# Mixtures taken out of PSUM two banks at a time, from a ring of three pairs, with the last bias among the matmuls

## The reference

```
x = x + L0(x)     # conditional 1x1: agg_w = einsum('bk,koi->boi', att, weight); out = agg_w @ x + att @ bias_k
x = x + L1(x)     # grouped convolution, 4 groups, 9 taps, pad 4, plus c_weight @ cond and a bias
x = x + L2(x)     # conditional 1x1, as L0 with its own weights
x = x + L3(x)     # conditional 1x1, as L0 with its own weights
att = softmax(gelu(gelu(cond @ W0 + b0) @ W1 + b1) @ W2 + b2)   # 8 shares for each sample and layer
```

## Time and profile before

| what | value |
|---|---|
| median of 3 runs | 484.26 us (484.23 to 484.34) |
| the profiled execution's own time | 484.1 us |
| span of its profile | 482.3 us |
| TensorE busy (matmul) | 473.2 us, 98% of the span |
| TensorE weight loads | 446.3 us, 93% |
| VectorE busy | 320.2 us, 66% |
| ScalarE busy | 248.5 us, 52% |
| GpSimd busy | 151.2 us, 31% |
| mean granted TensorE clock | 0.997 of full speed |

### The profile page before, as it was taken

How to read it: one execution, slowest core, us unless ns; L and a number is a source line. 1 busy time by engine, 2 the same in 40 slices (tenths; PEclk the granted TensorE clock), 3 DMA queues, 4 the chain that set the end, 5 groups by cost and what they waited for, 6 DMA issues and landing times.

```text
span 482.3 us, 17714 instructions
## 1 busy us (share of the span) xinstructions
PE 473.2 (98%) x8003; PEld 446.3 (93%) x8003; DVE 320.2 (66%) x409; ACT 248.5 (52%) x414; POOL 151.2 (31%) x151
## 2 busy tenths in 40 slices
PE   8989999999999999999999999999999999999996
PEld 7978999999999999999999999999999999999995
DVE  3548687767676876767687776767777676777424
ACT  5654445466544545654455466444545654455544
POOL 2935072324133322414331331333223142420110
PEclk9999999999999999999999999999999999999998
DMA  8696977676546476664746666464667746452224
GB/s 277 207 334 184 302 232 226 209 221 208 186 120 215 156 217 219 207 216 112 211 149 217 209 214 216 129 206 140 215 203 220 220 149 208 131 187 77 90 88 175
DMA packets 39244, 92.86 MB, mean 193 GB/s; under 512 B 4601, under 2 KB 25473, under 8 KB 35201
## 3 DMA queue, kind: packets, MB, share of 16 engines
q1 hardware_dynamic: 39168, 91.73, 60.5%
HBM read 53.95 MB, written 37.77 MB: 190 GB/s over the span
## 4 chain that ended last, share of the span: by engine, by line
PE 97%; DMA 1%; issue 1%; DVE 0%; SPq 0%; DVEq 0%
PE cv_ps L508 59%; PE aux_ps L488 18%; PE aux_ps L537 15%; PE cv_ps L444 2%; PE cv_ps L431 1%; DMA consts_sb<-in_consts_dram 1%; PE cv_ps L537 1%; PE aux_ps L431 1%; PE aux_ps L466 0%; DVE y_all L847 0%; DVE m_all L797 0%; PE aux_ps L455 0%; PE aux_ps L400 0%; SPq L318 0%; SPq L319 0%
## 5 line engine op out<-in xcount | busy, mean ns | idle before, releaser
L508 PE MATMUL cv_ps<-x_hi,conv_lo 32*128 32x512 f32 x1536 | 284.7, 391 | 0.0
L508 PE MATMUL cv_ps<-x_hi,conv_hi 32*128 32x512 f32 x1536 | 284.2, 389 | 0.0
L508 PE MATMUL cv_ps<-x_lo,conv_hi 32*128 32x512 f32 x1536 | 284.2, 391 | 0.0
L508 PEld LDWEIGHTS cv_ps<-x_lo,conv_hi 32*128 32x128 f32 x1536 | 172.5, 184 | 4.7
L508 PEld LDWEIGHTS cv_ps<-x_hi,conv_hi 32*128 32x128 f32 x1536 | 171.5, 183 | 5.6
L508 PEld LDWEIGHTS cv_ps<-x_hi,conv_lo 32*128 32x128 f32 x1536 | 172.4, 183 | 4.5
L779 DVE SCALAR_TENSOR_TENSOR x_lo<-cv_ps,d_all,x_hi 128x512 fp32r<-128x512 f32 x128 | 87.2, 744 | 132.4 <-ACT x_hi L626 132.4
L636 ACT ACTIVATE y_all<-aux_ps,e_all 128x512 f32<-128x512 f32 x122 | 74.0, 689 | 134.1 <-PE aux_ps L537 134.1
L626 ACT ACTIVATE x_hi<-cv_ps,d_all 128x512 fp32r<-128x512 f32 x128 | 77.5, 688 | 67.9 <-PE cv_ps L508 67.9
L488 PE MATMUL aux_ps<-x_hi,a_hi 32*128 32x512 f32 x512 | 99.5, 391 | 2.3 <-issue 2.3
L488 PE MATMUL aux_ps<-x_hi,a_lo 32*128 32x512 f32 x512 | 99.1, 388 | 0.0
(11 more groups left out here) (104 smaller groups left out, 455.5 us busy)
## 6 DMA issues: line engine op xcount, KB each, us to landing
x_sb<-in_x_dram SPq DMA_DIRECT2D x31, 1024.0 KB, 6.5
out_dram<-y_all SPq DMA_DIRECT2D x60, 512.0 KB, 7.4
a_rep<-a_pairs SPq DMA_DIRECT2D x64, 128.0 KB, 7.3
m_rep<-m_pairs SPq DMA_DIRECT2D x64, 128.0 KB, 6.1
out_dram<-y_all SPq DMA_DIRECT2D x8, 256.0 KB, 2.6
a_pairs<-a_all SPq DMA_DIRECT2D x1, 1920.0 KB, 12.4
m_pairs<-m_all SPq DMA_DIRECT2D x1, 1792.0 KB, 12.2
m_all<-in_mix_dram SPq DMA_DIRECT2D x2, 512.0 KB, 5.5
```

The source lines that it names most:

```text
L508: mm = pe.matmul(cv_ps[:, g, :], w[rows(g), j, :], a[n % 2][rows(g), q, s:s + T], start=(i == 0), stop=(i == steps - 1))
```

## The change

- The mixtures are taken out in pairs: pair r holds the mixtures 2r and 2r+1, in two neighbouring banks, and one instruction of 128x1024 takes both out once both are made. There are 12 pairs; ScalarE takes r = 0, 2, 4, 6, 7, 8 and 10, VectorE takes r = 1, 3, 5, 9 and 11.
- The ring has three pairs of banks, so six banks in place of seven (`MIX_RING` = 6). Mixture t waits for the pair of mixture t - 6.
- `bias_e` becomes a generator that runs as a fifth member of the round after the first 12 steps: four empty steps, then one matmul in each step. The second stop of the mixtures goes.
- `bias_d` is issued before TensorE waits for the shares, in place of between the two products of `attention`.
- The load of the convolution's weights is issued after the first save of the layer-0 weights.
- On GpSimd, `split_a0(0)` comes before the split of the convolution's weights in place of behind it.

```diff
-BY_SCALAR = [t % 2 == 0 or t in (9, 21) for t in range(MIXES)]
+TWO = 2
+BY_SCALAR = [r % 2 == 0 or r == 7 for r in range(MIXES // TWO)]
+E_BEHIND = 4
...
-        mix_ps = [*prep_ps, aux_ps[:, 2, :], aux_ps[:, 3, :], aux_ps[:, 0, :]]
-        MIX_RING = len(mix_ps)
+        mix_ps = [cv_ps[:, 2:4, :], cv_ps[:, 0:2, :], aux_ps[:, 2:4, :]]
+        MIX_RING = TWO * len(mix_ps)
...
         def mix_taken(t):
-            return mix_out_a if BY_SCALAR[t] else mix_out_v, sum(by == BY_SCALAR[t] for by in BY_SCALAR[:t + 1])
+            r = t // TWO
+            return mix_out_a if BY_SCALAR[r] else mix_out_v, sum(by == BY_SCALAR[r] for by in BY_SCALAR[:r + 1])
...
             sp.dma_start(w3_sb, w3.rearrange("p (k m) -> p k m", k=K)).then_inc(e_loaded, DMA)
-            sp.dma_start(conv_f[:], conv).then_inc(conv_loaded, DMA)
...
-            sp.wait_ge(*mix_taken(NOG - 2))
+            sp.wait_ge(*mix_taken(NOG - 1 - TWO))
             sp.wait_ge(*mix_taken(NOG - 1))
             save(a0_all, a0_dram, 0, 1, a0_saved[0])
+            sp.dma_start(conv_f[:], conv).then_inc(conv_loaded, DMA)
...
                     if MIX_RING <= t:
                         pe.wait_ge(*mix_taken(t - MIX_RING))
-                    elif t == MIX_RING - 1:
-                        pe.wait_ge(spread_ready, NL)
...
-            def bias_e(options):
+            def bias_e():
+                for _ in range(E_BEHIND):
+                    yield
+                pe.wait_ge(e_loaded, DMA)
+                pe.wait_ge(c2_att_ready, 1)
+                for n in range(1, NL):
+                    pe.matmul(e_ps, bias_sb[:, n, :], att_t[:, n, :], start=(n == 1), stop=False)
+                    yield
+                for k in range(K):
+                    mm = pe.matmul(e_ps, w3_sb[:, k, :], c2_att[:, k, :], start=False, stop=(k == K - 1))
+                    if k == K - 1:
+                        mm.then_inc(e_made, 1)
+                    yield
...
             fill(8)
+            bias_d()
             attention()
...
             in_turn(mixing, 3 * G)
             biases()
-            in_turn(mixing, 2 * G)
-            bias_e(range(0, 4))
-            in_turn(mixing)
-            bias_e(range(4, K)).then_inc(e_made, 1)
+            in_turn([*mixing, bias_e()])
...
-            def mix_evacuate(t):
-                act.wait_ge(mix_made, t + 1)
-                nc.scalar.activation(mix_columns(t), mix_bank(t), ACT.Identity).then_inc(mix_out_a, 1)
+            def mix_evacuate(r):
+                act.wait_ge(mix_made, TWO * (r + 1))
+                nc.scalar.activation(mix_columns(r), mix_banks(r), ACT.Identity).then_inc(mix_out_a, 1)
...
+            split_a0(0)
             pool.wait_ge(pool_chain, PH)
             nc.gpsimd.tensor_copy(conv_hi[:], conv_f[:]).then_inc(conv_split, 1)
...
-            split_a0(0)
             split_a0(1)
...
-            def mix_evacuate(t):
-                dve.wait_ge(mix_made, t + 1)
-                nc.vector.tensor_copy(mix_columns(t), mix_bank(t)).then_inc(mix_out_v, 1)
+            def mix_evacuate(r):
+                dve.wait_ge(mix_made, TWO * (r + 1))
+                nc.vector.tensor_copy(mix_columns(r), mix_banks(r)).then_inc(mix_out_v, 1)
```

More of the change, by code:

```diff
@@ L236, in cond_resid_kernel, with mix_banks, mix_columns @@
         RING = len(prep_ps)
-        mix_ps = [*prep_ps, aux_ps[:, 2, :], aux_ps[:, 3, :], aux_ps[:, 0, :]]
-        MIX_RING = len(mix_ps)
[L242 to L247, removed]
+        mix_ps = [cv_ps[:, 2:4, :], cv_ps[:, 0:2, :], aux_ps[:, 2:4, :]]
+        MIX_RING = TWO * len(mix_ps)
+        def mix_banks(r):
+            return mix_ps[r % len(mix_ps)].rearrange("p u c -> p (u c)").rearrange("p (x b o) -> p b x o", x=TWO * G, b=B)
+        def mix_columns(r):
+            layer, u = TWO * r // NOG, TWO * r % NOG
             to = a0_all if layer == 0 else a23_all[layer - 1]
-            return to[:, :, OG * u:OG * (u + 1)].rearrange("p b (j o) -> p b j o", j=G)
+            return to[:, :, OG * u:OG * (u + TWO)].rearrange("p b (x o) -> p b x o", x=TWO * G)
         def mix_taken(t):
-            return mix_out_a if BY_SCALAR[t] else mix_out_v, sum(by == BY_SCALAR[t] for by in BY_SCALAR[:t + 1])
+            r = t // TWO
+            return mix_out_a if BY_SCALAR[r] else mix_out_v, sum(by == BY_SCALAR[r] for by in BY_SCALAR[:r + 1])
         h_ps = [[cv_ps[:, h, 0:REPEAT * B]] + [aux_ps[:, 2 * h + n, 0:REPEAT * B] for n in range(NL - 1)] for h in range(2)]
@@ L401, in attention @@
                           eye_sb[0:NB, 0:NB], start=True, stop=True).then_inc(att_made, 1)
-                bias_d()
                 pe.matmul(att_t_ps.rearrange("k n b -> k (n b)"), shares[:, 0, :, 0], eye_sb[0:NB, 0:NB], start=True,
@@ L427, in mixtures @@
                         pe.wait_ge(*mix_taken(t - MIX_RING))
-                    elif t == MIX_RING - 1:
-                        pe.wait_ge(spread_ready, NL)
                     for j in range(G):
-                        mm = pe.matmul(mix_ps[t % MIX_RING][:, P * j:P * (j + 1)], mix_f[layer][rows(c), G * h + j, :],
+                        mm = pe.matmul(mix_ps[t // TWO % len(mix_ps)][:, t % TWO, P * j:P * (j + 1)], mix_f[layer][rows(c), G * h + j, :],
                                        spread[rows(c), layer].rearrange("p b o -> p (b o)"), start=True, stop=True)
@@ L438, in quad_product @@
                 if m == 0:
-                    pe.wait_ge(*mix_taken(MIXES - 2))
+                    pe.wait_ge(*mix_taken(MIXES - 1 - TWO))
                     pe.wait_ge(*mix_taken(MIXES - 1))
@@ L457, in biases @@
                 pe.matmul(c2_ps, bias_sb[:, 1, :], att_t[:, 1, :], start=True, stop=True).then_inc(c_made, 1)
-            def bias_e(options):
[L460 to L465, removed]
+            def bias_e():
[7 more added lines that the diff above has]
+                for k in range(K):
                     mm = pe.matmul(e_ps, w3_sb[:, k, :], c2_att[:, k, :], start=False, stop=(k == K - 1))
-                return mm
+                    if k == K - 1:
+                        mm.then_inc(e_made, 1)
+                    yield
             def layer0_steps(n, p):
@@ L642, in m_evacuate @@
                                      prep_ps[m % RING], ACT.Identity).then_inc(m_out, 1)
-            for t in range(MIXES):
-                if BY_SCALAR[t]:
-                    mix_evacuate(t)
+            for r in range(MIXES // TWO):
+                if BY_SCALAR[r]:
+                    mix_evacuate(r)
             for m in range(3):
@@ L812, in _ @@
             nc.vector.tensor_scalar(d_sb[:], d_ps, fside_sb, None, ALU.add).then_inc(d_ready, 1)
-            for t in range(2 * LANES):
-                if not BY_SCALAR[t]:
-                    mix_evacuate(t)
+            for r in range(LANES):
+                if not BY_SCALAR[r]:
+                    mix_evacuate(r)
             dve.wait_ge(c_made, 1)
@@ L820, in _ @@
                                     ALU.mult).then_inc(c2_att_ready, 1)
-            for t in range(2 * LANES, MIXES):
-                if not BY_SCALAR[t]:
-                    mix_evacuate(t)
+            for r in range(LANES, MIXES // TWO):
+                if not BY_SCALAR[r]:
+                    mix_evacuate(r)
             dve.wait_ge(e_made, 1)
```

## The result

The changed kernel takes 499.57 us (median of 4 runs, 498.79 to 502.07) against 484.3 us before: a ratio of 1.032, 95% interval 1.029 to 1.035. It is slower, in the direction forecast, but by 15 us where 7.7 were forecast, and outside the range given. The profiled execution took 502.07 us, with a span of 500.3 us; it is the longest of the four, so its account is 2.5 us larger than the median's.

A forecast was written before the change was run, and what follows sets the result against it. TensorE was taken to bound the kernel, with only the preparation changing: quad products +9.94 us, minus the 2.26 us wait, gave +7.7, so 491.8 profiled and 491.9 us forecast. The 8-in-10 range was 489.4 to 495.2.

The forecast's parts named there:

- What bounds the kernel: Whole kernel: TensorE is 97% of the chain of waits, so time changed ahead of the main part reaches the end.
- signs of being wrong: Preparation: overlapping takings-out, quad products before 28.5 or after 32.4, or granted clock below 1.00 before 40 us.
- The mixture ring: Mixtures: takings-out run one after another until the ninth turn; quad products start at 30.2 against 20.26, +9.9 us.
- Taking-out: Mixtures: emptying two PSUM banks in one instruction takes 1.06 us on ScalarE and 1.25 on VectorE.
- hand-over: Mixtures: from one pair's emptying, through TensorE's resumed matmuls, to the next pair's emptying: 0.68 us, between 0.58 and 0.77.
- the sum: Start of layer 0: +9.94 - 2.26 = +7.7 us, taking the profiled execution from 484.1 to 491.8.
- What was hidden: Preparation: bias work costs nothing extra; layer-0 weights are split by 31.0, so the 2.26 us wait goes completely.
- first question: Preparation: when the quad products can start, since the change gives back time only until TensorE resumes at 26.36.
- rival A: Mixtures: the ring does not serialize, layer 0 starts 2.3 us earlier, 481.8 us, or 484; chance 0.09.
- a matmul of the last bias adds 0.25: Mixture steps 22 to 25: each such matmul adds 0.25 us to a step of 0.22.
- rival B: Preparation: TensorE's clock falls to 1.2 GHz; quad products +3.8, nine hand-overs +2.7, giving 498 us; chance 0.08.
- The row that I held against B: Before layer 0: granted clock stayed 1.00 from 24.10 to 26.40, though TensorE was busy only 0.04 us.

The follow-up runs named there:

- the halves and idle matmuls: The changed kernel with the last bias in two halves and three idle matmuls ahead of each ring wait: 491.37, 491.95, 499.24 and 502.73 us.
- Pairs in step: The changed kernel with lanes 0 and 1 beginning together and lanes 2 and 3 two steps later: 494.77 us, ratio 1.019.
- the pairs undone: The changed kernel with mixtures taken out one bank at a time again, from seven banks, the other edits staying: 488.96 us, ratio 1.009.
- the pairs in step and the halves: The changed kernel with lanes 0 and 1 together, lanes 2 and 3 two steps later, and the last bias in two halves: 491.52 us, ratio 1.013.
- in step with halves and idle matmuls: The changed kernel with lanes begun two by two, last bias in two halves, three idle matmuls per ring wait: 490.18, 502.60, 503.21 and 503.54 us.
- the pairs alone: The kernel before with only the takings-out of two banks from a ring of three pairs: 496.88 us, ratio 1.025.
- halves: The changed kernel with nothing but the last bias in two halves as before: 496.49 us, ratio 1.025.

## Why the prediction was wrong

*What bounds the kernel* held: the main part is as full after as before, and the whole loss is in the first 45 us. Two of the prediction's own signs of being wrong came in: quad products later than 32.4 (38.27), and a clock below 1.00 before 40 us.

*The mixture ring* held, in mechanism and, at the full clock, in size. The order read from the code is in every trace with the pairs in the old order: no two takings-out overlap until the ninth turn. Taking-out was put at 1.06 and 1.25 us and measured 1.02 and 1.23; the hand-over at 0.68, measured 0.60 at the full clock. In the kernel with the halves and idle matmuls the nine turns took 15.77 us, and 16.23 were worked out. That its two short runs, 491.4 and 492.0 us, meet the 491.8 of the sum is luck in part: it began 0.4 us late, its turns and its end were 1.2 shorter, its quad products 1.3 longer, and layer 0's first stretch 0.5 shorter. Pairs in step shows, twice, that 5 us hang on the order and not on the width.

*What was hidden* held for the layer-0 weights: their split ended at 29.26, with 31.0 given as the latest, and the wait went. That it won nothing here is as forecast. The forecast's *first question*, when the quad products can start, was the right one. The 2.26 us that rival A counts as a plain gain didn't come: done alone, this part moved nothing in twelve runs.

*The first step that failed*, though not the dearer one, is the price of the last bias: "a matmul of the last bias adds 0.25", and of its first matmuls "nothing". The 0.25 came from eight records one behind the other. Among the lanes such a matmul uses all the rows that the lanes share; in the chain of the pairs undone the step's own records come first, then the bias's, and the next step starts only behind them (19.43, 19.86, 20.20). A step grew from 0.22 to 0.77 us at the full clock, by 0.55 and not by 0.25, and to 1.30 at the lower one. From pair 7 on TensorE, not the taking-out, set the turns. Measured cost in the changed kernel: 3.1 us. With that alone the forecast would have been 495.0, still inside its range.

*The second*, which took the time out of the range, is TensorE's clock: the sum has every term at the full clock, and the forecast left the lower one to rival B at 8 in 100. B is what happened. Its 0.3 more for each hand-over is what was measured (0.90 to 0.98 against 0.60); its +3.8 for the quad products measured +2.7, because the clock came back in them, at 44.0. The account of the profiled execution against the forecast's times: the ring begins at 12.25 and not 10.74 (+1.5: the first matmul of a mixture is 0.45 later, at 9.79 against 9.34, and the records up to the first taking-out take 2.44 us where they take 1.38 at the full clock); it reaches pair 9 in 19.5 us and not 16.2 (+3.3: hand-overs of 0.90 to 0.98, and two turns of 2.6); from pair 9 to the quad products 6.5 and not 3.2 (+3.3, steps of 1.3); the quad products 6.5 and not 3.8 (+2.7). Together 10.8, less 0.5 because layer 0's first stretch was shorter (3.00 against 3.48): 10.3, which is 502.07 - 491.8. Of the median's 15.3 us, the ring at the full clock is some 6.3 (the estimate of 490.6 against 484.3), the last bias 3.1 (499.57 against 496.49), and the rest, some 5.9, the clock (496.49 against 490.6, where the idle matmuls are the only other difference). These are estimates and they overlap, since the bias's price itself depends on the clock.
The row that I held against B, a clock still at 1.00 while TensorE idled for 2.3 us, was evidence of one short gap. It said nothing of the 30 us of the mixtures. By the Trainium skill (TensorE: Matmul & The Clock Gate, "A second HAM failure mode: psum-queue depth-cycling") frequent short waits for PSUM cost the clock; every kernel here with the ring of pairs and no idle matmuls ran most of its preparation at 0.50 (or, with the pairs in step and the halves, with records of that length), which agrees as far as it goes. But the short waits aren't shown to be the cause. With the pairs undone the clock fell as well, in the steps with the last bias, where TensorE had been busy 4.20 of 4.20 us from 17.0 to 21.2; it fell with six single banks too; and in the kernel in step with halves and idle matmuls it stayed low for 33.6 us in which TensorE was never idle by the trace.

*What stays open.* In the profile after, the clock fell at 9.9 us, before the first wait for the ring at 12.3; with the pairs alone at 15.6, with halves at 15.1. So why the clock falls stays open. What the traces do show is that wherever it fell among the mixtures it came back only in the quad products, with the ring of pairs (32.3 to 44.0) and with single banks (31.2 to 31.5); the ring makes that stretch longer. Why three of four runs of the pairs in step with idle matmuls took 12 to 13 us longer than the fourth wasn't settled. The split of 5.9 and 3.1 has no run behind it that changes the clock alone.

## What to carry to other kernels

Where the lanes of one queue share a ring, and the queue is worked through in order, look for the last instruction that a taking-out needs and the first wait for the one before it: if the wait stands ahead, every turn is serial, whatever the number of engines; merging two takings-out into one moves that point. A matmul that uses the whole array doesn't slip in among matmuls on a quarter of its rows: price it by a trace in which it does. And a stage that makes TensorE wait is to be priced twice, at either level of its clock, with what follows (here the quad products, 3.84 against 6.53 us).

## What the runs showed of the hardware that was not expected

- A granted clock of 1.00 in the views is no proof of the full clock in the preparation: in the kernel with the pairs in step and halves it is shown as 1.00 through the whole preparation, yet its eight idle matmuls at 6.9 us take 1.7 times what they take in the kernel before, and its quad products 6.25 us. The second row is the same group in the changed kernel:

```profile
6.87 2.08 PE L412 MATMUL cv_ps<-idle_sb 128*128 128x256 f32 x8
```
```profile
6.82 1.21 PE L412 MATMUL cv_ps<-idle_sb 128*128 128x256 f32 x8
```

- So a mean clock of 0.998 with 493.5 us and one of 0.987 with 487.6 us stand side by side in one kernel's runs: the length of a known group of matmuls is the better witness.
- Out of PSUM, 1024 columns over two banks take 1.02 us on ScalarE and 1.22 to 1.23 on VectorE, against 0.60 and 0.69 for 512: the width alone wins 0.15 to 0.18 us for each pair, and 0.06 against two single ones back to back (1.08 and 1.29).
- VectorE's splits of 1024 columns take 5.54 and 5.62 us for two beside GpSimd's work, against 1.22 for one before, and GpSimd's own 512-column cast 1.61 against 0.61. In both traces the first of the two ends 1.1 to 1.2 us, so one split's length, after GpSimd's `conv_lo` instruction (31.10 and 31.97), as if it had waited for that to end.
